# Edge stage of a graph kernel: zero columns widen the first layer's weights to 128, and one VectorE reduction over the three directions stands ahead of the flush

## The chip, the core and the metric

One NeuronCore of a Trainium2 chip runs the whole kernel as one program. Its engines run side by side, each with its own queue in program order, and wait for each other by semaphores: TensorE (PE, matmuls into PSUM), VectorE (DVE, elementwise and reductions), ScalarE (ACT), GpSimd (POOL, here mostly the issue of gathers and scatters) and SyncE (SP, which issues DMAs). The metric is the device time of one execution in microseconds (us), lower is better.

## What is computed

A layer over a graph of 6250 nodes with 256 features and 200000 edges sorted by their target: a layer norm, a graph convolution with a small network per edge, linear attention, and a mixture of eight experts. The part that matters here is the edge part of the convolution. Each edge has ten length features, from which two layers make 256 weights, and four attributes y. It fetches the row of its source node, 64 scalars g0 and 64 vectors g1 of three directions, and sends 512 values to its target node:

```python
h = jax.nn.silu(edge_length_embedded @ W_mlp1 / math.sqrt(N_BASIS))      # 10 -> 100
ew = h @ W_mlp2 / math.sqrt(N_HID)                                       # 100 -> 256
wa, wb, wc, wd = (ew[:, :MUL], ew[:, MUL:2 * MUL], ew[:, 2 * MUL:3 * MUL], ew[:, 3 * MUL:])
g0 = f0[edge_src]; g1 = f1[edge_src]
y0 = edge_attr[:, 0]; y1 = edge_attr[:, 1:4]
m0a = wa * g0 * y0[:, None]
m0b = wb * jnp.einsum('eum,em->eu', g1, y1) / math.sqrt(3.0)
m1a = wc[:, :, None] * g0[:, :, None] * y1[:, None, :]
m1b = wd[:, :, None] * g1 * y0[:, None, None]
s_mid = jax.ops.segment_sum(jnp.concatenate([m0a, m0b], axis=1), edge_dst, num_segments=N)
v_mid = jax.ops.segment_sum(jnp.concatenate([m1a, m1b], axis=1), edge_dst, num_segments=N)
```

The change touches `edge_length_embedded @ W_mlp1` and the `einsum` over the three directions m.

## The kernel before

The function `edges` works through 403 items. An item is 512 edges in four chunks of 128, one edge to a partition (GE = 512, GC = 4, MUL = 64, D = 256). Since edges are sorted, a chunk's targets lie in one block of 128 nodes, and the 49 blocks' sums stay in `acc` in SBUF. Items come in three phases, by how many blocks one spreads over: 355 items of one piece (the long phase), 35 of two pieces, 13 of four. In each phase a loop on the chip runs four items a turn, with buffers that rotate over two or four. The order on each engine is written out by hand, and the lead between engines is set by semaphore counts.

For item n the engines do this:

- SP loads the edges' records (`edge`) and the length features, transposed (`el`), which `prepare` and `nodes` have split in high and low parts, 30 rows of features in a tile of 128 partitions.
- POOL gathers the source nodes' rows, four indirect DMAs an item, into `rows[k]`.
- PE, `hidden` (L1005): the first layer, one matmul in rounded single precision. The stationary operand is `K.w_e1s`, 128 partitions by 100 columns, filled in its first 30 partitions by L335 and zero below; 512 edges stream past it into `ps_h`.
- ACT, `silu` (L876): reads 100 partitions of `ps_h` into `hT`.
- PE, `weights` (L1011): the second layer into `ps_e`, four full-precision matmuls, which the trace shows as two passes each.
- DVE, `one_hot` (L933): for each edge, where its target lies in its block. `by_attributes` (L942): g1 times y1, 768 products, into `dot3`, laid out as chunk, direction, channel. Channels lie side by side, so that one channel's three directions are 64 words apart. `second` (L948) adds directions 0 and 1 into `dot2`, and `third` (L952) adds direction 2 into `dot`. `products` (L958, L961, L965), called one item later, multiplies by the second layer's weights into `msg`. `flush` (L924) adds a finished block sum from PSUM (`ps_s`) to `acc`.
- ACT, `scalings` (L884) and `weighted` (L894): the parts that are scaled by one attribute per edge.
- PE, `sums` (L1024): the one-hot rows times the messages, into `ps_s`, for item n - 1.

In one turn, DVE runs: products of n - 1, one_hot of n, by_attributes of n, then the flushes. An item of the long phase has one flush, of n - 2, which waits for PE's sums of n - 2 (`summed`). The variable `at_end` says how many flushes stand ahead of the additions: at least one before. PE runs: weights of n, hidden of n + 1, sums of n - 1.

Some lines elsewhere are named by rows below. Two of them read SBUF with a step between elements. `place` (L1443, in `update`) is reduced over its eight experts with 11 words (44 bytes) from one to the next. The statistics that L381 subtracts are read with 6 words (24 bytes) between elements; L388 reads and writes the same number side by side. L1407 and L1472 reduce eight elements that lie side by side. L1700 is the experts' first layer, whose operands are rounded single precision, with 128 columns.

Of the kernel before, what the change touches and what calls it, by code (L numbers as in the profile page):

```python
# [19 lines left out]
P = 128  # L20
N_NODES, D, MUL = 6250, 256, 64
# [3 lines left out]
GE, GC = 512, 4  # L25
# [22 lines left out]
HID, BAS = 100, 10  # L48
# [14 lines left out]
f32, f32r, bf16, i32 = mybir.dt.float32, mybir.dt.float32r, mybir.dt.bfloat16, mybir.dt.int32  # L63
ALU, ACT, AX = mybir.AluOpType, mybir.ActivationFunctionType, mybir.AxisListType
# [49 lines left out]
class Mem:  # L114
# [5 lines left out]
    def sb(self, name, shape, dt=f32):  # L120
        return self.ctx.enter_context(self.nc.sbuf_tensor(f"{self.prefix}_{name}", shape, dt))
# [8 lines left out]
def prepare(nc, A, K):  # L130

    with ExitStack() as ctx:
        m = Mem(nc, ctx, "prepare")
        w_hi, low_row, w_part = m.sb("w_hi", [3 * BAS, HID], f32r), m.sb("low_row", [3 * BAS, 1]), m.sb("w_part", [3 * BAS, HID])
# [16 lines left out]
        made, scaled, d, summed, numbered, balanced = (m.sem(x) for x in (  # L151
            "made", "scaled", "vector_steps", "summed", "numbered", "balanced"))
# [84 lines left out]
        def _(dve):  # L237
            v, n = nc.vector, [0]
# [70 lines left out]
            spare = slice(2 * (QUADS + TWOS), NPAIR)  # L309
# [22 lines left out]
            nc.vector.scalar_tensor_tensor(w_part[:, :], w_hi[:, :].bitcast(f32), low_row[:, :], K.w_e1[:, :], ALU.mult,  # L332
                                           ALU.add).then_inc(scaled, 1)
            dve.wait_ge(scaled, 3)
            nc.vector.tensor_copy(K.w_e1s[0:3 * BAS, :], w_part[:, :]).then_inc(scaled, 1)  # L335
            nc.vector.tensor_scalar(K.sc_m[:, :], K.attr[:, :], C_S / 8.0, None, ALU.mult)
            dve.wait_ge(centred, 1)
            nc.vector.tensor_copy(K.w_kvT[:, :, 2 * D + E:], K.w_rc[:, :, :])
# [465 lines left out]
def edges(nc, A, K, acc):  # L804
# [3 lines left out]
    with ExitStack() as ctx:  # L808
# [3 lines left out]
        el, edge = four("el", [P, GE], f32r), four("edge", [P, GC, REC], i32)  # L812
        y = [e[:, :, 2:REC].bitcast(f32) for e in edge]
        hT = two("hT", [HID, GE])
        hot_y = two("hot_y", [P, GC, P])
        warm = m.sb("warm", [P, 1])
        spare = K.w_kvT[:, :, :].rearrange("p c n -> p (c n)")[:, 0:4 * D]
        dot3 = spare[:, 0:3 * GC * MUL].rearrange("p (c i u) -> p c i u", c=GC, i=3)
        dot2 = spare[:, 3 * GC * MUL:].rearrange("p (c u) -> p c u", c=GC)
        room = K.x2[:, :, :].rearrange("p t d -> p (t d)")  # L820
        rows = [room[:, k * GC * D:(k + 1) * GC * D].rearrange("p (c n) -> p c n", c=GC) for k in range(4)]
        left = room[:, 4 * GC * D:]
# [2 lines left out]
        dot = [left[:, k * GC * MUL:(k + 1) * GC * MUL].rearrange("p (c n) -> p c n", c=GC) for k in range(2)]  # L825
# [4 lines left out]
        loaded = [[m.sem(f"loaded_{ph.pieces}_{k}") for k in range(4)] for ph in PHASES]  # L830
        gathered = [m.sem(f"gathered{k}") for k in range(4)]
        c = {x: m.sem(x) for x in ("padded", "cleared", "messages", "flushed", "hidden", "act", "weights", "outer", "scaled",
                                   "hot_y", "dot3", "dot2", "dot", "hot", "summed", "passed")}
        block = ctx.enter_context(nc.Block())
        records = lambda ph: 16 * 3 * ph.pieces
        arrived = lambda ph, n, k: (loaded[PHASES.index(ph)][k], ph.loads(n, k, records(ph)))
# [73 lines left out]
        @block.vector  # L910
        def _(dve):
            v = nc.vector
            dve.sem_inc(c["messages"], FREE)
            dve.sem_inc(c["flushed"], FREE)
            for k in range(4):
                v.memset(el[k][:, :].bitcast(f32), 0.0).then_inc(c["padded"], 1)
            v.memset(acc[:, 0:(NB + 1) // 2, :], 0.0).then_inc(c["cleared"], 1)
            dve.wait_ge(c["cleared"], 2)

            def flush(n, k, ph, j, b):  # L920
                dve.wait_ge(c["flushed"], ph.seq(n) + (j + FREE))
                dve.wait_ge(c["summed"], ph.seq(n) + (j + 1 + AHEAD))
                a = acc[:, bass.ds(b, 1), :].rearrange("p a n -> p (a n)")
                v.tensor_tensor(a, a, ps_s[ph.bank(k, j)][:, :], ALU.add).then_inc(c["flushed"], 1)  # L924

            def homes(n, ph, pieces):
                return load_values(nc, mybir.EngineType.DVE, K.item_block, ph.seq(n) + pieces[0], len(pieces), NB)

            def one_hot(n, k, ph, j):
                at = slice(j * ph.len, (j + 1) * ph.len)  # L930
                if j == 0:
                    dve.wait_ge(*arrived(ph, n, k))
                v.scalar_tensor_tensor(hot[k][:, at, :], K.iota_f[:, :].unsqueeze(1).to_broadcast([P, ph.len, P]),  # L933
                                       K.item_base[:, bass.ds(ph.seq(n) + j, 1)],
                                       edge[k][:, at, 1:2].to_broadcast([P, ph.len, P]),
                                       ALU.add, ALU.is_equal).then_inc(c["hot"], 1)

            def by_attributes(n, k):
                dve.wait_ge(gathered[k], per(n, k, 64, 4))
                if not (isinstance(n, int) and n == 0):  # L940
                    dve.wait_ge(c["dot"], n)
                v.tensor_tensor(dot3[:, :, :, :], rows[k][:, :, MUL:D].rearrange("p c (i u) -> p c i u", i=3),  # L942
                                y[k][:, :, 1:4].unsqueeze(3).to_broadcast([P, GC, 3, MUL]),
                                ALU.mult).then_inc(c["dot3"], 1)

            def second(n):
                dve.wait_ge(c["dot3"], n + 1)
                v.tensor_tensor(dot2[:, :, :], dot3[:, :, 0, :], dot3[:, :, 1, :], ALU.add).then_inc(c["dot2"], 1)  # L948

            def third(n, k):  # L950
                dve.wait_ge(c["dot2"], n + 1)
                v.tensor_tensor(dot[k % 2][:, :, :], dot2[:, :, :], dot3[:, :, 2, :], ALU.add).then_inc(c["dot"], 1)  # L952

            def products(n, k):
                f, g = rows[k], msg[k % 2]
                w = ps_e[k % 2][:, :].rearrange("p (c b u) -> p c b u", c=GC, b=4)
                dve.wait_ge(c["weights"], n + 1)
                v.tensor_tensor(g.rearrange("p c (b u) -> p c b u", u=MUL)[:, :, 0:MSG // MUL:8, :],  # L958
                                f[:, :, 0:MUL].unsqueeze(2).to_broadcast([P, GC, 2, MUL]), w[:, :, 0:4:3, :],
                                ALU.mult).then_inc(c["outer"], 1)  # L960
                v.tensor_tensor(g[:, :, MUL:D].rearrange("p c (i u) -> p c i u", i=3),  # L961
                                f[:, :, MUL:D].rearrange("p c (i u) -> p c i u", i=3),
                                w[:, :, 1:2, :].to_broadcast([P, GC, 3, MUL]), ALU.mult)
                dve.wait_ge(c["dot"], n + 1)
                v.tensor_tensor(g[:, :, D:D + MUL], dot[k % 2][:, :, :], w[:, :, 2, :], ALU.mult).then_inc(c["messages"], 1)  # L965

            def body(n, k, of):
                if not (isinstance(n, int) and n < 1):
                    products(n - 1, (k - 1) % 4)
                for j in range(of(0).pieces):  # L970
                    one_hot(n, k, of(0), j)
                by_attributes(n, k)
                earlier, newer = [], []
                if not (isinstance(n, int) and n < 2):
                    earlier = [(n - 2, (k - 2) % 4, of(-2), j) for j in range(of(-2).early, of(-2).pieces)]
                if not (isinstance(n, int) and n < 1):
                    newer = [(n - 1, (k - 1) % 4, of(-1), j) for j in range(of(-1).early)]
                flushes = earlier + newer
                if flushes:
                    m, _, ph, j = flushes[0]  # L980
                    blocks = load_values(nc, mybir.EngineType.DVE, K.item_block, ph.seq(m) + j, len(flushes), NB)
                    flushes = [f + (b,) for f, b in zip(flushes, blocks)]
                at_end = max(len(earlier) if newer else len(earlier) - 1, 1)
                for f in flushes[:at_end]:
                    flush(*f)
                second(n)
                third(n, k)
                for f in flushes[at_end:]:
                    flush(*f)

            item_steps(dve, 0, NI, body, 2)
            products(NI - 1, (NI - 1) % 4)
            for n, first in ((NI - 2, ONE.early), (NI - 1, 0)):
                blocks = load_values(nc, mybir.EngineType.DVE, K.item_block, ONE.seq(n) + first, ONE.pieces - first, NB)
                for j, b in enumerate(blocks):
                    flush(n, n % 4, ONE, first + j, b)

        @block.tensor
        def _(pe):
            t = nc.tensor  # L1000

            def hidden(n, k, ph):

                pe.wait_ge(*arrived(ph, n, k))
                t.matmul(ps_h[k % 2][0:HID, :], K.w_e1s[:, :], el[k][:, :], start=True, stop=True).then_inc(c["hidden"], 1)  # L1005

            def weights(n, k):
                pe.wait_ge(c["messages"], n + 3)
# [853 lines left out]
def program(nc, A, out):  # L1862
    with ExitStack() as ctx:
# [16 lines left out]
        K.w_nodeA, K.w_nodeB = sb("w_nodeA", [P, 256]), sb("w_nodeB", [P, 256])  # L1880
        K.w_kvT, K.w_qT, K.w_projT = sb("w_kvT", [P, 2, 2 * D + 2 * E]), sb("w_qT", [P, 2, 256]), sb("w_projT", [P, 2, 256])
        K.w_e1, K.w_e2 = sb("w_e1", [3 * BAS, HID]), sb("w_e2", [HID, 256])
        K.w_e1s = sb("w_e1s", [P, HID], f32r)
        K.w_lo, K.w_rc, K.w_pr, K.b_pr = sb("w_lo", [P, 4, LO]), sb("w_rc", [P, 2, E]), sb("w_pr", [P, 2, E]), sb("b_pr", [P, E])
        K.z, K.std = sb("z", [P, NT, 2 * E]), sb("std", [P, NT])
        K.w_r, K.b_r, K.b_proj = sb("w_r", [P, 2, E]), sb("b_r", [P, E]), sb("b_proj", [P, D])
# [92 lines left out]
```

## Time and profile before

| | us |
|---|---|
| median of three runs | 3426.73 |
| lowest and highest | 3422.16, 3427.67 |
| the profiled execution | 3423.07 |
| its span, first to last instruction | 3421.3 |
| the long phase, from its first product to its last | 286.7 to 2207.9 |
| the phase of two pieces | 2213.3 to 2393.2 |
| the phase of four pieces | 2399.5 to 2492.1 |

A profile is one execution: 1.8 us of it lie around the span. A row names its line in the kernel before, the engine, the operation, the tiles written and read, and shapes as partitions by elements. PEld is PE's weight load, which overlaps its matmuls. The names in the trace are those of the memory that is used: `k_w_kvT` in the edge stage is the room of `dot3` and `dot2`, and `k_x` that of rows, messages, `dot` and one-hot rows. Matmul ends are modelled, and so is how early a matmul may seem to start; the starts of the weight loads are firmer. A DVE instruction that waits for nothing starts a little ahead of the recorded end of the one in front, so distances between starts add up, not durations. DVE's instructions without work in the tiles (register operations, loads of a table entry) run ahead beside the engine's work.

### The profile page before, as it was taken

The numbers are of one execution on the slowest core, as the hardware profiler recorded it, in microseconds if no ns is written. First come the engines' busy times: TensorE is split into PE (matmuls) and PEld (weight loads), VectorE is DVE, ScalarE is ACT, GpSimd is POOL, SyncE is SP. The second block draws the span as 40 slices with busy tenths as digits, with TensorE's granted clock in tenths as the row PEclk, the third lists the DMA queues.
The fourth block names the chain that finished last, engine by engine and source line by source line (L and its number), as shares of the span: only waits on it lengthen the run. The fifth ranks groups of instructions, "written<-read, shape, count | busy, mean of one in ns | idle before, by whom it ended". The sixth has DMA issues, their size and how long they took to land. (4 is left out here: it accounts for less than half of the span.)

```text
span 3421.3 us, 65304 instructions
## 1 busy us (share of the span) xinstructions
PE 3271.9 (96%) x15915; PEld 2833.8 (83%) x15915; DVE 2718.1 (79%) x5058; ACT 2630.4 (77%) x8258; POOL 2292.5 (67%) x2140
## 2 busy tenths in 40 slices
PE   5998999999999999999999999999789499999998
PEld 4886888888888888888888888888679388888887
DVE  7868889998889888898888988999967556656521
ACT  6667888888888888888888888888656367666742
POOL 5746777777777777777777777777527545445533
PEclk8998999999999999999999999999999799999999
DMA  6963333333333333333333333444348444545544
GB/s 221 308 228 98 111 110 111 110 110 110 110 111 111 111 110 110 111 111 111 110 110 111 111 111 110 110 109 108 84 118 160 140 119 139 144 117 143 141 109 132
DMA packets 322226, 431.91 MB, mean 126 GB/s; under 512 B 129227, under 2 KB 249751, under 8 KB 313943
## 3 DMA queue, kind: packets, MB, share of 16 engines
q0 software_dynamic: 105936, 253.72, 27.5%
q1 hardware_dynamic: 216199, 177.13, 17.6%
q8 instruction: 39, 0.64, 0.1%
q14 instruction: 52, 0.43, 0.0%
HBM read 366.03 MB, written 64.59 MB: 126 GB/s over the span
## 5 line engine op out<-in xcount | busy, mean ns | idle before, releaser
L864 POOL DMA_INDIRECT k_x<-gather_table,edges_edge x1612 | 1692.4, 1050 | 524.0 <-issue 493.8
L884 ACT ACTIVATE k_x<-k_x,edges_edge 128x64 f32<-128x64 f32 x4836 | 1196.8, 334 | 58.2 <-DVE k_x L958 54.8
L1024 PE MATMUL edges_ps_sum<-k_x,edges_hot_y 128*128 128x256 f32 x3224 | 961.9, 380 | 24.8 <-DVE accumulators L924 22.3
L1024 PE MATMUL edges_ps_sum<-k_x 128*128 128x256 f32 x3224 | 960.6, 380 | 0.0
L1011 PE MATMUL edges_ps_edge<-k_w_e,edges_hT 100*128 100x256 f32 x3224 | 765.4, 380 | 9.1 <-ACT edges_hT L876 9.1
L1024 PEld LDWEIGHTS edges_ps_sum<-k_x,edges_hot_y 128*128 128x128 f32 x3224 | 612.1, 190 | 131.3 <-DVE accumulators L924 19.3
L1011 PEld LDWEIGHTS edges_ps_edge<-k_w_e,edges_hT 100*128 100x128 f32 x3224 | 613.0, 190 | 96.2 <-issue 10.3
L1024 PEld LDWEIGHTS edges_ps_sum<-k_x 128*128 128x128 f32 x3224 | 613.2, 190 | 84.4
L894 ACT ACTIVATE edges_hot_y<-k_x,edges_edge 128x128 f32<-128x128 f32 x1612 | 514.2, 390 | 5.5 <-DVE k_x L933 5.3
L924 DVE TENSOR_TENSOR accumulators<-accumulators,edges_ps_sum 128x512 f32 x477 | 327.0, 686 | 162.4 <-PE edges_ps_sum L1024 158.1
L876 ACT ACTIVATE edges_hT<-edges_ps_hidden 100x512 f32<-100x512 f32 x403 | 240.0, 596 | 248.3 <-PE edges_ps_hidden L1005 247.9
L942 DVE TENSOR_TENSOR k_w_kvT<-k_x,edges_edge 128x768 f32<-128x768 f32 x403 | 386.5, 959 | 2.1 <-DMA k_x<-gather_table,edges_edge 2.1
L961 DVE TENSOR_TENSOR k_x<-k_x,edges_ps_edge 128x768 f32<-128x768 f32 x403 | 381.5, 947 | 0.0
L1778 ACT ACTIVATE experts_g<-experts_ps_h,weights_constants 128x512 f32<-128x512 f32 (+1 forms) x256 | 163.3, 638 | 255.1 <-PE experts_ps_h L1700 255.1
L1815 DVE TENSOR_TENSOR experts_g_lo<-experts_g,experts_g_hi 128x512 fp32r<-128x512 f32 x192 | 132.5, 690 | 226.9 <-ACT experts_g_hi L1778 226.9
L933 DVE SCALAR_TENSOR_TENSOR k_x<-k_iota_f,k_item_base,edges_edge 128x512 f32<-128x512 f32 (+2 forms) x477 | 309.7, 662 | 0.0
L1648 POOL DMA_INDIRECT out<-experts_y,weights_rows x112 | 198.8, 1775 | 157.1 <-DVE experts_y L1832 125.0
L958 DVE TENSOR_TENSOR k_x<-k_x,edges_ps_edge 128x512 f32<-128x512 f32 x403 | 276.6, 686 | 28.4 <-issue 0.2
L1638 POOL DMA_INDIRECT k_x<-tokens,weights_rows x112 | 129.4, 1155 | 233.6 <-DMA weights_rows<-slots 184.2
L1005 PE MATMUL edges_ps_hidden<-edges_el,k_w_e1s 128*100 128x512 f32 x403 | 236.6, 587 | 6.6 <-DMA edges_el<-el_parts 6.6
L952 DVE TENSOR_TENSOR k_x<-k_w_kvT 128x256 f32<-128x256 f32 x403 | 171.3, 425 | 13.7
L948 DVE TENSOR_TENSOR k_w_kvT<-k_w_kvT 128x256 f32<-128x256 f32 x403 | 168.6, 418 | 0.1
(329 smaller groups left out, 4362.5 us busy)
## 6 DMA issues: line engine op xcount, KB each, us to landing
k_x<-in_w SPq DMA_DIRECT2D x64, 1024.0 KB, 7.0
k_x<-gather_table,edges_edge POOLq DMA_INDIRECT x1612
el_parts<-nodes_el_parts SPq DMA_DIRECT2D x41, 384.0 KB, 3.5
edges_el<-el_parts SPq DMA_DIRECT2D x355, 40.0 KB
edges_el<-el_parts SPq DMA_DIRECT2D x425, 20.0 KB
nodes_el<-in_el SPq DMA_DIRECT2D x41, 192.0 KB, 3.9
k_x<-in_x SPq DMA_DIRECT2D x7, 896.0 KB, 11.1
residual<-nodes_res SPq DMA_DIRECT2D x49, 128.0 KB, 3.5
```

The lines of the kernel that those rows point to most:

```text
L864: nc.gpsimd.indirect_dma_start(out=rows[k][:, j, :], out_offset=None, in_=K.table_d.rearrange("t p d -> (t p) d"), in_offset=bass.Indirect ...
L876: nc.scalar.activation(hT[k % 2][:, :], ps_h[k % 2][0:HID, :], ACT.Silu, scale=1 / math.sqrt(BAS)).then_inc(c["act"], 1)
L884: x = nc.scalar.activation(g[:, j, D + MUL * (i + 1):D + MUL * (i + 2)], g[:, j, 2 * D:MSG], ACT.Identity, scale=y[k][:, j, 1 + i:2 + i])
L894: x = nc.scalar.activation(hot_y[k % 2][:, j, :], hot[k][:, j, :], ACT.Identity, scale=y[k][:, j, 0:1])
L924: v.tensor_tensor(a, a, ps_s[ph.bank(k, j)][:, :], ALU.add).then_inc(c["flushed"], 1)
L933: v.scalar_tensor_tensor(hot[k][:, at, :], K.iota_f[:, :].unsqueeze(1).to_broadcast([P, ph.len, P]), K.item_base[:, bass.ds(ph.seq(n) + j, ...
L942: v.tensor_tensor(dot3[:, :, :, :], rows[k][:, :, MUL:D].rearrange("p c (i u) -> p c i u", i=3), y[k][:, :, 1:4].unsqueeze(3).to_broadcast ...
L958: v.tensor_tensor(g.rearrange("p c (b u) -> p c b u", u=MUL)[:, :, 0:MSG // MUL:8, :], f[:, :, 0:MUL].unsqueeze(2).to_broadcast([P, GC, 2, ...
L961: v.tensor_tensor(g[:, :, MUL:D].rearrange("p c (i u) -> p c i u", i=3), f[:, :, MUL:D].rearrange("p c (i u) -> p c i u", i=3), w[:, :, 1: ...
L1005: t.matmul(ps_h[k % 2][0:HID, :], K.w_e1s[:, :], el[k][:, :], start=True, stop=True).then_inc(c["hidden"], 1)
L1011: x = t.matmul(ps_e[k % 2][:, j * 256:(j + 1) * 256], hT[k % 2][:, j * P:(j + 1) * P], K.w_e2[:, :], start=True, stop=True)
L1024: x = t.matmul(into[:, o * D:(o + 1) * D], rows_hot[:, j, :], msg[k % 2][:, j, o * D:(o + 1) * D], start=j % ph.len == 0 and o == 0, stop= ...
```

## The change

Three edits. The stationary operand of the first layer gets 28 more columns, all zero, and the matmul writes 128 partitions of `ps_h` rather than 100; ACT still reads 100. The additions `second` and `third` become one `tensor_reduce` over `dot3`, viewed with the direction innermost. And `at_end` may be zero, so that in the long phase the flush stands behind the reduction.

```diff
-            nc.vector.tensor_copy(K.w_e1s[0:3 * BAS, :], w_part[:, :]).then_inc(scaled, 1)
+            nc.vector.tensor_copy(K.w_e1s[0:3 * BAS, 0:HID], w_part[:, :]).then_inc(scaled, 1)
...
-        dot2 = spare[:, 3 * GC * MUL:].rearrange("p (c u) -> p c u", c=GC)
...
-            def second(n):
+            def over_directions(n, k):
                 dve.wait_ge(c["dot3"], n + 1)
-                v.tensor_tensor(dot2[:, :, :], dot3[:, :, 0, :], dot3[:, :, 1, :], ALU.add).then_inc(c["dot2"], 1)
-
-            def third(n, k):
-                dve.wait_ge(c["dot2"], n + 1)
-                v.tensor_tensor(dot[k % 2][:, :, :], dot2[:, :, :], dot3[:, :, 2, :], ALU.add).then_inc(c["dot"], 1)
+                v.tensor_reduce(dot[k % 2][:, :, :], dot3.rearrange("p c i u -> p c u i"), AX.X, ALU.add).then_inc(c["dot"], 1)
...
-                at_end = max(len(earlier) if newer else len(earlier) - 1, 1)
+                at_end = max(len(earlier) if newer else len(earlier) - 1, 0)
                 for f in flushes[:at_end]:
                     flush(*f)
-                second(n)
-                third(n, k)
+                over_directions(n, k)
                 for f in flushes[at_end:]:
                     flush(*f)
...
-                t.matmul(ps_h[k % 2][0:HID, :], K.w_e1s[:, :], el[k][:, :], start=True, stop=True).then_inc(c["hidden"], 1)
+                t.matmul(ps_h[k % 2][:, :], K.w_e1s[:, :], el[k][:, :], start=True, stop=True).then_inc(c["hidden"], 1)
...
-        K.w_e1s = sb("w_e1s", [P, HID], f32r)
+        K.w_e1s = sb("w_e1s", [P, P], f32r)
```

On DVE, in the loop of the long phase, from the products by attributes of one item to the first product with the weights. The rows are before's, then after's; L799 loads a table entry, and `accumulators` is `acc`:

```order
L942 TENSOR_TENSOR k_w_kvT<-k_x,edges_edge 128x768 [waits edges_dot,edges_gathered3]
L799 ISA
L799 TENSOR_LOAD k_item_block
L921 REGISTER_ALU
L924 ISA [waits edges_summed,edges_flushed]
L924 TENSOR_TENSOR accumulators<-accumulators,edges_ps_sum 128x512
L948 TENSOR_TENSOR k_w_kvT<-k_w_kvT 128x256 [waits edges_dot3]
L952 TENSOR_TENSOR k_x<-k_w_kvT 128x256 [waits edges_dot2]
L958 TENSOR_TENSOR k_x<-k_x,edges_ps_edge 128x4x2x64 [waits edges_weights]
```

```order
L941 TENSOR_TENSOR k_w_kvT<-k_x,edges_edge 128x768 [waits edges_dot,edges_gathered3]
L799 ISA
L799 TENSOR_LOAD k_item_block
L947 TENSOR_REDUCE k_x<-k_w_kvT 128x256 [waits edges_dot3]
L920 REGISTER_ALU
L923 ISA [waits edges_summed,edges_flushed]
L923 TENSOR_TENSOR accumulators<-accumulators,edges_ps_sum 128x512
L953 TENSOR_TENSOR k_x<-k_x,edges_ps_edge 128x4x2x64 [waits edges_weights]
```

The wait for `summed` and the flush behind it have moved past the addition over directions, which waits only for `dot3`, DVE's own product just in front.

On DVE, in the loop of the two-piece phase, from the first flush of an item to the next item's first product, before and after:

```order
L924 TENSOR_TENSOR accumulators<-accumulators,edges_ps_sum 128x512
L947 REGISTER_ALU
L948 TENSOR_TENSOR k_w_kvT<-k_w_kvT 128x256 [waits edges_dot3]
L952 TENSOR_TENSOR k_x<-k_w_kvT 128x256 [waits edges_dot2]
L921 REGISTER_ALU
L924 ISA [waits edges_summed,edges_flushed]
L924 TENSOR_TENSOR accumulators<-accumulators,edges_ps_sum 128x512
```

```order
L923 TENSOR_TENSOR accumulators<-accumulators,edges_ps_sum 128x512
L946 REGISTER_ALU
L947 TENSOR_REDUCE k_x<-k_w_kvT 128x256 [waits edges_dot3]
L920 REGISTER_ALU
L923 ISA [waits edges_summed,edges_flushed]
L923 TENSOR_TENSOR accumulators<-accumulators,edges_ps_sum 128x512
```

Here nothing has changed its place: one flush ahead of the addition, one behind it. PE's order is the same in both kernels.

## Rows read from the trace of the kernel before

**Rows 1.** Page, part 1: busy us, share of the span, instructions.

```profile
PE 3271.9 (96%) x15915; PEld 2833.8 (83%) x15915; DVE 2718.1 (79%) x5058; ACT 2630.4 (77%) x8258; POOL 2292.5 (67%) x2140
```

**Rows 2.** By window: length, busy of PE, PEld, DVE, ACT, POOL (count), PEclk, DMA.

```profile
1000.00:1500.00 500.00, 500.00 (x2310) 436.02 (x2309) 449.95 (x740) 436.63 (x1569) 387.54 (x370) 1.00 0.40 111
...
2208.00:2397.00 189.00, 189.00 (x874) 164.77 (x873) 186.77 (x347) 163.88 (x592) 143.34 (x137) 1.00 0.41 109
2397.00:2500.00 103.00, 78.25 (x329) 62.69 (x329) 91.55 (x180) 59.43 (x220) 50.02 (x48) 0.97 0.27 70
```

**Rows 3.** Waits from 300 to 2200 us: us in total, times, longest.

```profile
ACT edges_hT L876 <- PE edges_ps_hidden L1005: 240.0, 351, 0.7
DVE accumulators L924 <- PE edges_ps_sum L1024: 150.9, 351, 0.5
```

**Rows 4.** DVE's timeline, one long-phase item: start us, us, what, [idle before].

```profile
1503.87 0.69 DVE L958 TENSOR_TENSOR k_x<-k_x,edges_ps_edge 128x512 f32<-128x512 f32 x1
...
1506.33 0.97 DVE L942 TENSOR_TENSOR k_w_kvT<-k_x,edges_edge 128x768 f32<-128x768 f32 x1
1507.67 0.69 DVE L924 TENSOR_TENSOR accumulators<-accumulators,edges_ps_sum 128x512 f32 x1 [0.37 <-PE edges_ps_sum L1024]
1508.28 0.42 DVE L948 TENSOR_TENSOR k_w_kvT<-k_w_kvT 128x256 f32<-128x256 f32 x1
1508.73 0.42 DVE L952 TENSOR_TENSOR k_x<-k_w_kvT 128x256 f32<-128x256 f32 x1
1509.29 0.69 DVE L958 TENSOR_TENSOR k_x<-k_x,edges_ps_edge 128x512 f32<-128x512 f32 x1
```

**Rows 5.** L958 in the long and the two-piece phase: durations, first and last start.

```profile
L958 DVE TENSOR_TENSOR k_x<-k_x,edges_ps_edge x356: 680/687/689, 286.7 to 2207.9; 128x512 f32<-128x512 f32 x178
...
L958 DVE TENSOR_TENSOR k_x<-k_x,edges_ps_edge x34: 677/679/689, 2213.3 to 2393.2; 128x512 f32<-128x512 f32 x34
```

**Rows 6.** Timeline of DVE, one item of the two-piece phase.

```profile
2348.22 0.41 DVE L948 TENSOR_TENSOR k_w_kvT<-k_w_kvT 128x256 f32<-128x256 f32 x1
...
2349.02 0.68 DVE L924 TENSOR_TENSOR accumulators<-accumulators,edges_ps_sum 128x512 f32 x1
2349.61 0.68 DVE L958 TENSOR_TENSOR k_x<-k_x,edges_ps_edge 128x512 f32<-128x512 f32 x1
```

**Rows 7.** Reductions by shape: busy us, mean ns of one, idle time before.

```profile
L1443 DVE TENSOR_REDUCE update_where<-k_w_qT 128x10 f32<-128x80 f32 x7 | 2.1, 295 | 0.2
...
L1407 DVE TENSOR_REDUCE update_best<-k_iota_f 128x5 f32<-128x40 f32 x7 | 1.4, 197 | 0.2
...
L1472 DVE TENSOR_REDUCE k_w_e<-k_item_start 1x40 f32<-1x320 f32 x1 | 0.5, 474 | 0.0
L1443 DVE TENSOR_REDUCE update_where<-k_w_qT 128x6 f32<-128x48 f32 x2 | 0.5, 232 | 0.1
...
L1407 DVE TENSOR_REDUCE update_best<-k_iota_f 128x3 f32<-128x24 f32 x2 | 0.4, 177 | 0.1
```

**Rows 8.** The same view: reads with a step (L381) and side by side (L388).

```profile
L381 DVE TENSOR_TENSOR first_diff<-first_stats 128x49 f32<-128x49 f32 x1 | 0.2, 245 | 0.0
...
L388 DVE SCALAR_TENSOR_TENSOR first_var<-first_var,first_diff 128x49 f32<-128x49 f32 x1 | 0.2, 211 | 0.0
```

**Rows 9.** Timeline around the hidden layer; the experts' first layer, its weight load.

```profile
1508.87 0.17 PEld L1005 LDWEIGHTS edges_ps_hidden<-edges_el,k_w_e1s 128*100 128x100 f32 x1
...
1509.09 0.42 PEld L1024 LDWEIGHTS edges_ps_sum<-k_x,edges_hot_y 128*128 128x128 f32 x2
...
1509.32 0.59 PE L1024 MATMUL edges_ps_sum<-k_x,edges_hot_y 128*128 128x256 f32 x2
...
3000.14 0.39 PE L1700 MATMUL experts_ps_h<-experts_x_lo,experts_w_hi 128*128 128x512 f32 x1
3000.37 0.39 PE L1700 MATMUL experts_ps_h<-experts_x_hi,experts_w_lo 128*128 128x512 f32 x1
...
L1700 PEld LDWEIGHTS experts_ps_h<-experts_x_hi,experts_w_hi 128*128 128x128 f32 x384 | 72.7, 189 | 18.9 <-DVE experts_x_lo L1808 4.5
```

More of the change, by code:

```diff
@@ L832, in edges @@
         c = {x: m.sem(x) for x in ("padded", "cleared", "messages", "flushed", "hidden", "act", "weights", "outer", "scaled",
-                                   "hot_y", "dot3", "dot2", "dot", "hot", "summed", "passed")}
+                                   "hot_y", "dot3", "dot", "hot", "summed", "passed")}
         block = ctx.enter_context(nc.Block())
```

## The prediction

> **What bounds the kernel now.** The page's totals come first: TensorE (PE) is busy 96% of the span, VectorE (DVE) 79% [rows 1]. The share is an average over stages, so the table by windows comes next. From 1000 to 1500 us, in the middle of the edge stage, PE is busy all 500 us at granted clock 1.00 (the 2.4 GHz level), and DVE 449.95 us. In the two short phases behind it DVE is busy 186.77 of 189 and 91.55 of 103 us [rows 2]. So the edge stage has two limits: PE in its long phase of whole items, and DVE, all but full, in the phases of two and four pieces.
>
> The waits say how much room DVE has in the long phase. Between 300 and 2200 us PE stands in none of the waits. DVE waits 150.9 us for the sums that `flush` adds, 351 times, and ACT 240.0 us for the hidden layer [rows 3]. The timeline of one item shows where: the product L942 starts at 1506.33 and ends at 1507.30, then DVE is idle for 0.37 until the sums of item n-2 are done, flushes at 1507.67, adds at 1508.28 (L948) and 1508.73 (L952), and starts the next item's products (L958) at 1509.29, 5.42 us after the last start at 1503.87 [rows 4]. Over the long phase 356 starts of L958 lie between 286.7 and 2207.9 us, 5.41 us apart. In the two-piece phase 34 starts are 5.45 us apart [rows 5].
>
> **The two additions become one reduction.** L948 (0.42) and L952 (0.42) go, with the `dot2` hand-over between them. What comes is one `tensor_reduce` over 768 elements in, 256 out. Its input is `dot3` read with the direction innermost, and two directions of one channel lie 64 words, 256 bytes, apart. Its time D is the question of this change, and no row has this form. Both ends come from the nearest rows.
> - If the step costs nothing: reductions whose input lies side by side, L1407, take 177 ns for 24 elements and 197 for 40, and L1472 474 for 320, so 277/280 = 0.99 ns for each further element [rows 7]. That gives 197 + 728 x 0.99 = 0.92 us. The three-direction products, 768 elements, take 0.95 to 0.97 [rows 4]. I take 0.95 as this end.
> - If every step to another place costs: L1443 reduces with elements 44 bytes apart, and takes 232 ns for 48 and 295 for 80, so 63/32 = 1.97 ns an element, twice the other rate [rows 7]. That gives 295 + 688 x 1.97 = 1.65 us. With exactly twice the 1.04 ns by which the first additions (0.42 for 256) and the products (0.95 for 768) differ, (0.95 - 0.42)/512, it is 295 + 688 x 2.07 = 1.72.
>
> A second family of rows speaks for the step as the cause, not the reduction: L381 subtracts two columns of a table that has 24 bytes from element to element, 245 ns for 49 elements, while L388 with its elements side by side takes 211 [rows 8]. That is 34 ns more for 49 elements, near one more DVE step each less a smaller fixed part. The steps seen are 24 and 44 bytes and both cost; 256 bytes is farther, not nearer, so I take D = 1.70 us, between 1.60 and 1.80.
>
> Two pages of the Trainium skill pull apart here. "Advanced Engine Details and Errata", section "SBUF Cachelines", says that an access pattern needs at least two hits on a 16-byte line to run at full rate, which 24, 44 and 256 bytes all miss; by that rule the sum would be the forecast below, and the rows of L1443 agree. "VectorE: DVE Perf Modes", section "The perf-mode tier table", puts `tensor_reduce` at one element a cycle like an fp32 `tensor_tensor`, with no word on the step; by that rule it would be the first rival, and only the rows with side-by-side input agree.
>
> **The sum for DVE in the long phase.** The order shows that the reduction now stands straight behind L942, and the flush behind it, so that the 0.37 of waiting is filled by work. One item of DVE without any wait is then:
> - L958 to the start of L942: 1506.33 - 1503.87 = 2.46 [rows 4];
> - L942 with the hand-over of `dot3`: 0.97 + 0.03, the 0.03 being the gap between the end of L948 at 1508.70 and L952, which has the same kind of wait [rows 4]: 1.00;
> - the reduction until the flush starts: D less the 0.08 by which a follower that waits for nothing starts ahead of the recorded end (the flush of 0.69 is followed after 0.61) [rows 4]: 1.62;
> - the flush until the next L958: 0.60, from 2349.02 to 2349.61 [rows 6].
> Together 5.68 us, against the 5.41 that PE needs. DVE becomes the bound, by 0.27 us an item. 355 items: **+96 us**. The point from which DVE decides is D = 1.43. Had the additions stayed two, this order would give 2.46 + 1.00 + 0.80 + 0.60 = 4.86 and nothing on the path.
>
> Does a ring through the other engines need more than 5.68? ACT is held by its own work for 5.42 less the 0.68 that it waits per item (240.0/351) [rows 3], 4.74 us. The flush of item n-2 waits for sums that PE starts a whole item earlier, and PE's sums wait for a flush one item older still. Neither closes before DVE.
>
> **The two short phases.** There DVE is the bound already, and the order around the additions is as before: one or two flushes ahead, the others behind. From L948 to the next flush is 2349.02 - 2348.22 = 0.80 [rows 6]. It becomes D - 0.08 = 1.62, so +0.82 on each of 35 + 13 = 48 items: **+39 us**. PE's own waits there are for DVE, and grow with it.
>
> **The first layer with 128 columns.** PE's array takes 512 moving columns as before; only the weight load grows, from 0.17 us for 100 columns [rows 9] to the 0.19 of the other loads of 128 columns, rounded single-precision ones too (L1700, 189 ns) [rows 9]. It lies beside a matmul: one PE slot is 500/2310 = 0.216 us [rows 2]. The hidden layer's slot is 0.23, from 1509.09, where the next weights start, to 1509.32, and the experts' matmuls of the same type with full 128 columns are also 0.23 apart, 3000.14 to 3000.37 [rows 9]. So I take nothing; the bounds are 403 x 0.015 = 6 us gained, if the slot fell to 0.216, and 403 x 0.02 = 8 us lost, if the longer load showed. Both count only while PE is the bound, which it then is not. The zero columns' outputs land in rows of PSUM that no one reads. The Trainium skill ("TensorE: Matmul & The Clock Gate", "Weight-path perf modes") loads full 128-column weights faster when they aren't FP32; L1700's 189 ns shows no such thing for this type, and by that rule the sum would be no other, as the load is hidden.
>
> The order on the other queues is untouched. SP and POOL wait for `messages` and `scaled`, which follow DVE's pace: POOL's four gathers an item are not the bound: among the waits of the long phase none is for them [rows 3]. The wider weights are cleared once, ahead of everything.
>
> **Sum.** 96 + 39 = +135 us on the profiled 3423.07: 3558. The median of the runs is 3.7 above that execution, so I forecast **3562 us**. With D = 1.60 it is 0.17 x 355 + 0.72 x 48 = +95, with D = 1.80 0.37 x 355 + 0.92 x 48 = +175: 3522 to 3602 for this case.
>
> **Rivals.**
> 1. The step costs nothing (D = 0.95). DVE's item is 4.93, PE stays the bound, the long phase doesn't move. The short phases pay (0.95 - 0.08 - 0.80) x 48 = +3 us, and the wider weights give back up to 6: 3424 to 3430, no difference that can be told. For it: the L1407 and L1472 rows. Against it: L1443, which is the only reduction here with a step in SBUF, and L381. 0.14.
> 2. Part of the step is hidden, because three addresses return to neighbouring words for the next channel (D from 1.1 to 1.5). The long phase pays nothing up to D = 1.43. At 1.3: 0.42 x 48 = +20, so 3447; at 1.5: 0.07 x 355 + 0.62 x 48 = +55, so 3481. 0.06.
> 3. A step of 256 bytes is dearer than one of 44, by a third DVE step an element: D = 295 ns + 688 x 3.1 = 2.43 us, item 6.41, +1.00 x 355 + 1.55 x 48 = +429, 3856. Nothing in the rows shows that the price grows with the step. 0.04.
> 4. Rival 1 with more than 6.9 us saved on PE: the slot would have to fall by more than 0.015. 0.02.
>
> **How the numbers follow.** My forecast has 0.74. The range has to reach down through rival 2 to leave out 0.20: 3450 to 3610. 0.2% of this kernel, 7 us, is about what a measurement can tell from no change. Slower by more: 0.74 + 0.06 + 0.04 = 0.84; within it 0.14; faster 0.02.
>
> **What would show it.** Right: the reduction's row has 1.6 to 1.8 us; the flush has no idle time ahead of it; starts of the first product are 5.6 to 5.8 apart in the long phase, and DVE has next to no idle time there, while PE's busy share falls below 100%. Wrong at its root: the reduction takes under 1.43 us. Wrong in the sum: D as said, but DVE still waits, or its other operations change their times. For the weights: the load's row reads 0.19 and the slot around the hidden layer stays 0.23.

## The result and the profile after

| | before | after |
|---|---|---|
| median of 20 runs each, us | 3426.22 | 3430.09 |
| ratio, 95% interval | | 1.0017 (1.001 to 1.0023) |
| profiled execution, its span | 3423.07, 3421.3 | 3427.01, 3425.3 |

The kernel is 0.17% slower: less than the 0.2% that the forecast called no change, though twenty runs of each put it clear of zero. The forecast was 3562 us, 4% slower, within 3450 to 3610. The change that it forecast is 35 times the one measured, and the measured time lies below its range. One of the eleven executions of the kernel below that has the additions back in its short phases took 9232 us; its ratio is worked out without that one (median 3424.65).

The difference lies in the duration of the reduction, which takes 1.03 us and not 1.70. First the page's part 5 after, and the waits from 300 to 2200 us, which answer [rows 3]:

```profile
L947 DVE TENSOR_REDUCE k_x<-k_w_kvT 128x256 f32<-128x768 f32 x403 | 416.0, 1032 | 12.3
...
ACT edges_hT L875 <- PE edges_ps_hidden L999: 239.9, 351, 0.7
DVE k_x L953 <- PE edges_ps_edge L1005: 119.2, 351, 0.3
```

DVE no longer waits for the sums ahead of the flush. It waits for PE's second layer instead, ahead of the item's first product, 351 times as before, for 119 us rather than 151. DVE's timeline after, one item, answers [rows 4]; the last two rows are of the two-piece phase:

```profile
1504.50 0.69 DVE L953 TENSOR_TENSOR k_x<-k_x,edges_ps_edge 128x512 f32<-128x512 f32 x1 [0.34 <-PE edges_ps_edge L1005]
...
1506.96 0.95 DVE L941 TENSOR_TENSOR k_w_kvT<-k_x,edges_edge 128x768 f32<-128x768 f32 x1
1507.95 1.03 DVE L947 TENSOR_REDUCE k_x<-k_w_kvT 128x256 f32<-128x768 f32 x1
1508.90 0.68 DVE L923 TENSOR_TENSOR accumulators<-accumulators,edges_ps_sum 128x512 f32 x1
...
2347.55 0.68 DVE L923 TENSOR_TENSOR accumulators<-accumulators,edges_ps_sum 128x512 f32 x1
2348.15 0.68 DVE L953 TENSOR_TENSOR k_x<-k_x,edges_ps_edge 128x512 f32<-128x512 f32 x1
```

Read by starts: 2.46 from the first product to the products by attributes, 0.99 to the reduction, 0.95 to the flush. From a flush to the next item's first product it is 0.60 where DVE waits for nothing, as in the two-piece phase. That makes 5.00 in all. PE needs 5.42. Starts of the first product in the long phase (without its last one), in the two-piece and in the four-piece phase; the first two answer [rows 5]:

```profile
L953 DVE TENSOR_TENSOR k_x<-k_x,edges_ps_edge x355: 675/687/689, 286.9 to 2203.1; 128x512 f32<-128x512 f32 x178
...
L953 DVE TENSOR_TENSOR k_x<-k_x,edges_ps_edge x34: 667/669/686, 2213.9 to 2398.5; 128x512 f32<-128x512 f32 x34
...
L953 DVE TENSOR_TENSOR k_x<-k_x,edges_ps_edge x13: 678/680/681, 2404.8 to 2498.4; 128x512 f32<-128x512 f32 x13
```

The long phase runs at 5.41 us an item, as before. In the two-piece phase 33 steps take 184.6 us, against 179.9: 5.59 an item rather than 5.45. The last item's first product starts at 2498.4 rather than 2492.1, 6.3 us later, which is within the interval of the ratio (3.4 to 7.9 us). The span is only 4.0 longer. The missing 2.3 lie behind the edge stage, in code that didn't change: from that start to the span's end it is 926.9 us here and 929.2 before, and between 925.8 and 933.2 in the nine kernels, with and without the change, that run the same code there. DVE's busy time by windows answers [rows 2]: 465.29 of 500 us in the long phase, up from 449.95, and 188.59 of 189 in the two-piece one, up from 186.77.

```profile
1000.00:1500.00 500.00, 500.00 (x2310) 438.15 (x2309) 465.29 (x647) 436.46 (x1568) 387.25 (x370) 1.00 0.40 111
2208.00:2397.00 189.00, 189.00 (x854) 159.59 (x852) 188.59 (x305) 157.39 (x577) 145.80 (x134) 1.00 0.40 106
```

### The profile page after: what moved, and what is told of

The parts are those of the page before. It is cut to its first block and busy times, and to the rows that moved or that the text cites. A ratio compares the mean times of both kernels' runs of the same rounds, so it can differ in the third digit from the quotient of the medians.

```text
span 3425.3 us, 64989 instructions
## 1 busy us (share of the span) xinstructions
PE 3275.3 (96%) x15915; PEld 2841.0 (83%) x15915; DVE 2786.1 (81%) x4655; ACT 2628.4 (77%) x8258; POOL 2298.4 (67%) x2140
## 5 line engine op out<-in xcount | busy, mean ns | idle before, releaser
L947 DVE TENSOR_REDUCE k_x<-k_w_kvT 128x256 f32<-128x768 f32 x403 | 416.0, 1032 | 12.3
L999 PE MATMUL edges_ps_hidden<-edges_el,k_w_e1s 128*128 128x512 f32 x403 | 236.5, 587 | 6.4 <-DMA edges_el<-el_parts 6.4
L960 DVE TENSOR_TENSOR k_x<-k_x,edges_ps_edge 128x256 f32<-128x256 f32 x403 | 166.5, 413 | 0.0
```

The lines of the kernel that those rows point to most:

```text
L947: v.tensor_reduce(dot[k % 2][:, :, :], dot3.rearrange("p c i u -> p c u i"), AX.X, ALU.add).then_inc(c["dot"], 1)
```

## The experiments

**Was the sum right and only the duration wrong?** One addition of 576 elements on DVE ahead of each reduction, whose result nothing reads, makes up what the reduction lacked of 1.70.

```diff
                 dve.wait_ge(c["dot3"], n + 1)
+                v.tensor_tensor(filler[:, :], spare[:, 0:576], spare[:, 0:576], ALU.add)
                 v.tensor_reduce(dot[k % 2][:, :, :], dot3.rearrange("p c i u -> p c u i"), AX.X, ALU.add)...
```

> The changed kernel with one addition over 576 elements on DVE ahead of each reduction, its result read by no one. It stands for a reduction that takes 0.67 us more, that is 1.70 us, the duration the prediction had assumed. In the changed kernel DVE's item without waits is 2.46 + 0.99 + 0.95 + 0.60 = 5.00 us against PE's 5.42. If the sum of the prediction was right and only the duration was wrong: 5.00 + 0.67 = 5.67, +0.25 x 355 + 0.67 x 48 = +121 us over the changed kernel, so 3551 us, ratio to before 1.036. If DVE has more room than the sum says (its gaps hide part of it): under 1.02. If a ring through other engines closes: over 1.045.

Measured: 3545.45 us, ratio 1.0358 (1.0342 to 1.0374). The starts in the long phase:

```profile
L955 DVE TENSOR_TENSOR k_x<-k_x,edges_ps_edge x356: 672/680/692, 288.6 to 2296.2; 128x512 f32<-128x512 f32 x178
...
1000.00:1500.00 500.00, 494.40 (x2213) 412.72 (x2212) 496.97 (x708) 408.16 (x1501) 392.35 (x354) 1.00 0.38 106
```

355 steps in 2007.6 us are 5.655 us an item, against the 5.67 of the sum. The second row is the window from 1000 to 1500 us: DVE is busy 496.97 of 500, and PE falls to 494.40. The sum and its bound held, and no longer chain of waits through other engines showed.

**Where is the point from which DVE decides?** The same with 264 elements.

> As the filler run, with an addition over 264 elements, whose result no one reads, ahead of each reduction. It lasts 0.35 us from start to start. The sum of the prediction puts the point from which DVE decides in the long phase at 5.42 - 5.00 = 0.42 us more than the changed kernel has. So the long phase stays at 5.42 us an item and only the 48 items of the short phases pay: 0.35 x 48 = +17 us over the changed kernel, about 3443, ratio 1.0065. If the point lies lower (DVE needs some slack to keep PE fed), the long phase rises too: at half the slack 355 x 0.14 = 50 us more, ratio 1.02.

Measured: 3449.23 us, ratio 1.0071 (1.0057 to 1.0086). The starts in the long and in the two-piece phase, and the window from 1000 to 1500 us:

```profile
L955 DVE TENSOR_TENSOR k_x<-k_x,edges_ps_edge x356: 675/687/689, 288.1 to 2210.7; 128x512 f32<-128x512 f32 x178
...
L955 DVE TENSOR_TENSOR k_x<-k_x,edges_ps_edge x34: 675/682/683, 2216.1 to 2411.9; 128x512 f32<-128x512 f32 x34
...
1000.00:1500.00 500.00, 500.00 (x2310) 438.21 (x2309) 496.81 (x740) 437.08 (x1572) 387.54 (x370) 1.00 0.40 110
```

1922.6/355 = 5.416 in the long phase: 0.35 us of work more an item cost nothing there, with 0.07 left. In the two-piece phase 195.8/33 = 5.93, 0.34 up on the changed kernel. DVE is busy 496.81 of 500 us in the long phase and PE still all 500, so 0.07 us of slack an item is enough.

**Where does the small loss come from?** The additions are put back in the two short phases alone.

```diff
-            def over_directions(n, k):
+            def over_directions(n, k, ph):
                 dve.wait_ge(c["dot3"], n + 1)
+                if ph.pieces > 1:
+                    v.tensor_tensor(dot2[:, :, :], dot3[:, :, 0, :], dot3[:, :, 1, :], ALU.add).then_inc(c["dot2"], 1)
+                    dve.wait_ge(c["dot2"], n + 1 - QUADS)
+                    v.tensor_tensor(dot[k % 2][:, :, :], dot2[:, :, :], dot3[:, :, 2, :], ALU.add).then_inc(c["dot"], 1)
+                    return
...
```

> The changed kernel, but in the two short phases (35 + 13 items) the two additions are back, so that the reduction stands in the long phase alone. Theory 1, the loss of the changed kernel is the 0.15 us by which the reduction is longer (0.95 from start to start, against 0.80 for the two additions) on the 48 items where DVE is the bound: these items fall back to 5.45 us in the two-piece phase, and the ratio to before is 1.000 (within 0.0007), 6 us under the changed kernel. Theory 2, the loss comes from the long phase (the later flush, or the wider weights): the ratio stays at 1.0017.

Measured: 3425.82 us, ratio 1.0001 (0.9992 to 1.0011). In the two-piece phase:

```profile
L959 DVE TENSOR_TENSOR k_x<-k_x,edges_ps_edge x34: 678/680/686, 2213.8 to 2393.5; 128x512 f32<-128x512 f32 x34
```

179.7/33 = 5.45, as before. Reduction, later flush and wider weights all stay in for 355 items and cost nothing that can be told; the loss was the reduction in the 48 items of the short phases.

**The parts alone.** First the 128 columns.

> The kernel before with the first layer's weights widened to 128 columns and nothing else. Theory 1: the hidden layer's slot on PE doesn't change (0.23 us from the next weight load to the next matmul), the load takes 0.19 rather than 0.17 beside another matmul, ratio 1.000. Theory 2, the slot shrinks to the 0.216 of the other matmuls: 5.40 us an item in the long phase, 6 us gained, ratio 0.998. Theory 3, the longer load shows: 8 us lost, 1.002.

Measured: 3424.97 us, ratio 1.0006 (0.9996 to 1.0017). The interval leaves out the 0.998 of theory 2, and the 1.002 of theory 3 only narrowly. The trace says more: the long phase keeps 5.41 us an item, and the load takes 190 ns in the window from 1000 to 1500 us, where it took 167 before:

```profile
L1005 PEld LDWEIGHTS edges_ps_hidden<-edges_el,k_w_e1s 128*128 128x128 f32 x93 | 17.7, 190 | 2.4
...
1509.96 0.19 PEld L1005 LDWEIGHTS edges_ps_hidden<-edges_el,k_w_e1s 128*128 128x128 f32 x1
1510.18 0.43 PEld L1024 LDWEIGHTS edges_ps_sum<-k_x,edges_hot_y 128*128 128x128 f32 x2
```

The next weight load starts 0.22 us later, as before (1508.87 and 1509.09), so the longer load lies beside a matmul, and the slot didn't shrink either. Theories 2 and 3 are out.

Then the later flush, in the kernel before:

```diff
-                at_end = max(len(earlier) if newer else len(earlier) - 1, 1)
+                at_end = max(len(earlier) if newer else len(earlier) - 1, 0)
```

> The kernel before, with its two additions and 100 columns, in which only the flush of the long phase goes behind the additions. DVE's item without waits is 2.46 + 1.00 + 0.80 + 0.60 = 4.86 us against PE's 5.42. The wait of 0.37 us ahead of the flush disappears, and one of some 0.5 us comes ahead of the next first product, for PE's second layer. Theory 1: nothing moves, 5.416 us an item, ratio 1.000 (within 0.001). Theory 2, the later flush costs something at the phase borders or frees PE somewhere: a difference of over 0.1%.

Measured: 3425.15 us, ratio 1.0005 (0.9996 to 1.0014), and 5.41 us an item in the long phase. The wait moved as expected (waits from 300 to 2100 us):

```profile
DVE k_x L958 <- PE edges_ps_edge L1011: 160.9, 332, 0.5
```

**Why is the reduction cheap?** A block in which DVE alone reduces data in SBUF, in many shapes, stands between the edge stage and the next. `side` takes groups of r elements side by side. `apart` takes g groups of r elements that lie s words apart, while the groups are neighbours.

```diff
+            def side(g, r, op=ALU.add):
+                done(v.tensor_reduce(to[:, 0:g], flat[:, 0:g * r].rearrange("p (g r) -> p g r", r=r), AX.X, op))
+
+            def apart(g, r, s, op=ALU.add, src=flat, at=0):
+                done(v.tensor_reduce(to[:, 0:g], src[:, at:at + r * s].rearrange("p (r s) -> p s r", r=r)[:, 0:g, :], AX.X, op))
...
```

> The changed kernel with one more block between the edge stage and the next, in which DVE alone runs some 50 small reductions and additions on SBUF data, twice over, each waiting for the one before; the other engines stand still. Only their durations count, not the time of the run (some 25 us longer). The changed kernel's reduction took 1.03 us, 1.04 ns an element, though its three directions are 256 bytes apart, while L1443 of the kernel before took 1.97 ns for each further element at 44 bytes. Theory A, the step itself costs but only some steps: groups of 8 with 44 bytes rise by 2 ns an element here too, and groups with 256 bytes by 1 ns, so a step that keeps to whole 64 bytes is free. Theory B, the step never costs and L1443 is slowed by what the other engines do at its time: all forms rise by 1.0 ns an element, and 10 groups of 8 at 44 bytes take 0.20 us, like 10 groups side by side (0.24 at most). Theory C, the number of steps in a group counts, since three addresses come back to the neighbouring word soon: 8 at 256 bytes rise by 2 ns an element, 3 at 256 bytes by 1 ns, and between 3 and 16 it turns. In all of them the copy of the edge stage's form (4 x 64 groups of 3) takes 1.03.

Measured, groups by shape with mean ns. L1061 is `side`, L1064 `apart`, and L1088 a copy of the edge stage's form. The L1064 rows shown have a step of 256 bytes:

```profile
L1064 DVE TENSOR_REDUCE probe_to<-k_x 128x64 f32<-128x768 f32 x2 | 2.9, 1452 | 0.1
...
L1088 DVE TENSOR_REDUCE probe_to<-k_w_kvT 128x256 f32<-128x768 f32 x2 | 2.1, 1032 | 0.1
L1064 DVE TENSOR_REDUCE probe_to<-k_x 128x64 f32<-128x512 f32 x2 | 2.1, 1027 | 0.1
L1061 DVE TENSOR_REDUCE probe_to<-k_x 128x256 f32<-128x768 f32 x2 | 1.9, 954 | 0.1
L1064 DVE TENSOR_REDUCE probe_to<-k_x 128x40 f32<-128x320 f32 x2 | 1.4, 697 | 0.1
L1061 DVE TENSOR_REDUCE probe_to<-k_x 128x64 f32<-128x512 f32 x2 | 1.4, 686 | 0.1
...
L1061 DVE TENSOR_REDUCE probe_to<-k_x 128x40 f32<-128x320 f32 x2 | 1.0, 487 | 0.1
```

Groups of 8 with a step take 1027 ns for 64 groups where 686 are needed side by side: 5.3 ns more a group. 256 groups of 3 take 1032 against 954: 0.3 ns a group. Ten groups of 8 take 285 to 291 ns at 44, 48, 64, 128 and 256 bytes alike. So theory A, by which some steps are free for their size, is out. Theory B is out too: from 2511 to 2544 us, the time of this block, no other engine is busy, and L1443's form still costs more than side by side. It costs 1.6 ns an element for its sizes, and 1.72 for larger ones, (1027 - 697)/192, rather than 1.97. What is left is the number of steps in a group.

The second block asks what about that number counts. `lines` is `apart` with the groups q words from each other.

```diff
+            def lines(g, r, s, q):
+                a = flat[:, 0:r * s].rearrange("p (r g q) -> p g r q", r=r, q=q)[:, 0:g, :, 0]
+                done(v.tensor_reduce(to[:, 0:g], a, AX.X, ALU.add))
...
```

> The changed kernel with the same kind of block of DVE reductions as before, again read by their durations alone (the run is longer by the block). The first table showed, beyond the 1.04 ns an element of side-by-side input: groups of 8 at any step from 44 to 256 bytes cost 5.2 ns more a group, groups of 12 7.8, groups of 16 10.2, but groups of 3 only 0.3. Theory R (revisits): what costs is to go to another 16 bytes than those read just before; a few such lines stay at hand, so with 3 steps each line serves four groups, with 8 it is lost before the next group comes. Then groups of 3 whose neighbours are 16 bytes apart (each access a new line) cost some 0.65 ns an element more, 64 groups about 125 ns, and groups of 8 cost the same with neighbours 4, 8, 16 or 32 bytes apart. Between 3 and 8 steps there is a turn within one or two sizes. Theory G (group): every element of a group past the third or so costs 0.65 ns more, whatever was read before: groups of 3 cost nothing with neighbours 16 or 32 bytes apart either, and the extra of groups of 2 to 8 rises in a straight line from 3 on.

Measured, 64 groups each, side by side (L1061) and with a step of 256 bytes (L1064) in turn, from the timeline, for groups of 3, 4 and 8:

```profile
2510.62 0.35 DVE L1061 TENSOR_REDUCE probe_to<-k_x 128x64 f32<-128x192 f32 x1
2511.01 0.37 DVE L1064 TENSOR_REDUCE probe_to<-k_x 128x64 f32<-128x192 f32 x1
2511.41 0.42 DVE L1061 TENSOR_REDUCE probe_to<-k_x 128x64 f32<-128x256 f32 x1
2511.87 0.59 DVE L1064 TENSOR_REDUCE probe_to<-k_x 128x64 f32<-128x256 f32 x1
...
2516.76 0.69 DVE L1061 TENSOR_REDUCE probe_to<-k_x 128x64 f32<-128x512 f32 x1
2517.48 1.03 DVE L1064 TENSOR_REDUCE probe_to<-k_x 128x64 f32<-128x512 f32 x1
```

Groups of 3 pay 0.02 us for 192 elements, groups of 4 pay 0.17 for 256, 0.65 ns an element, and all larger ones pay about that rate too (8: 0.34/512). That is a jump between 3 and 4, not a line that rises from 3. And groups of 3 whose neighbours are 8, 16 and 32 bytes apart, rather than 4; the last row has neighbours at 4 bytes again:

```profile
2519.73 0.43 DVE L1068 TENSOR_REDUCE probe_to<-k_x 128x64 f32<-128x192 f32 x1
2520.20 0.50 DVE L1068 TENSOR_REDUCE probe_to<-k_x 128x64 f32<-128x192 f32 x1
2520.73 0.49 DVE L1068 TENSOR_REDUCE probe_to<-k_x 128x64 f32<-128x192 f32 x1
...
2530.16 0.37 DVE L1064 TENSOR_REDUCE probe_to<-k_x 128x64 f32<-128x192 f32 x1
```

At 16 bytes every access goes to 16 bytes not read before, and the groups of 3 pay as well: 0.15 us, 0.76 ns an element, near the 125 ns that theory R gave. Theory G is out. In `lines` the step inside a group grows with the distance of the neighbours, to 1024 bytes at 16, but the step isn't the reason: the last row has that step too, and takes 0.37 us. The cost rises from neighbours at 4 bytes over 8 to 16 and no further at 32, which is why the unit is taken to be 16 bytes. The reading that fits all these rows is theory R: what costs is a read from 16 bytes that aren't among the three read last. `dot3` with its three directions reads each of its three places four times in turn. That the engine keeps such places is inferred from the durations alone.

**Can both reads and writes be had side by side?** `dot3` as chunk, channel, direction: the product writes with a step of 12 bytes, and the reduction reads without.

> The changed kernel with the three products of a channel side by side in dot3, so that the reduction reads without a step and the product L941 writes with a step of 12 bytes. By the first table the reduction falls from 1.03 to 0.95 us, and the product rises by 75 ns for every 256 elements, 0.22 us, to 1.17 (seen for one addition over 256 elements written at 12 bytes: 499 ns against 424). So DVE's item is 0.14 us longer: nothing in the long phase (5.14 against 5.42), +7 us in the short phases, ratio to before 1.0037. If writing with a step is free where three passes fill the same places, the product stays at 0.95, 0.08 x 48 = 4 us come back and the ratio is 1.0006.

Measured: 3437.82 us, ratio 1.0039 (1.0027 to 1.0051). In the long phase, 1000 to 1500 us, and DVE's waits for gathered rows in the two-piece phase, 2215 to 2408 us:

```profile
L941 DVE TENSOR_TENSOR k_w_kvT<-k_x,edges_edge 128x768 f32<-128x768 f32 x93 | 112.4, 1209 | 0.0
L947 DVE TENSOR_REDUCE k_x<-k_w_kvT 128x256 f32<-128x768 f32 x93 | 88.6, 953 | 3.2
...
DVE k_w_kvT L941 <- DMA k_x<-gather_table,edges_edge: 3.9, 6, 0.7
```

The reduction fell by 0.08, and the product rose from 0.95 to 1.21, a little more than expected. The item of the two-piece phase rose by 0.26 us in the mean. Of this, 0.13 is the two operations by their starts: 27 of the 33 steps are 5.70 to 5.75 us long, against 5.59. The other six are 6.40 to 6.53 long, because DVE waits there for gathered rows, 3.9 us in all, 0.12 an item. In the changed kernel such a wait came once in this phase, for 0.4 us. Whether the new layout brings these waits about or this one execution is not shown.

**An attempt at a better kernel.** On top of the later flush, the four-piece phase runs flush, addition, flush, addition, flush, flush.

> The same, and in the four-piece phase the four flushes of an item are spread: flush, addition, flush, addition, flush, flush. Two flushes in a row are 0.82 us apart there, since the second waits for the first, but 0.60 when another operation follows. Theory 1, DVE's own chain is the bound of this phase as of the two-piece one: an item falls by 0.22 us or a little more, from 7.63 to 7.4, 13 items, 3 us less, ratio 0.999. Theory 2, the phase hangs on a ring between PE and DVE (PE waits for a flush to free a bank, DVE for the sums): bringing the second flush behind an addition delays PE and nothing is gained or 0.1 us an item is lost, ratio 1.000.

Measured: 3425.22 us, ratio 1.0004 (0.9994 to 1.0014). The first items of the phase wait for other engines and take up to 10.8 us here and 10.4 before, so the last nine are compared. Here are their first products, before and in this kernel, and this kernel's waits for the sums from 2431 to 2496 us:

```profile
L958 DVE TENSOR_TENSOR k_x<-k_x,edges_ps_edge x9: 678/680/680, 2433.2 to 2492.1; 128x512 f32<-128x512 f32 x9
...
L958 DVE TENSOR_TENSOR k_x<-k_x,edges_ps_edge x9: 679/681/682, 2435.7 to 2494.3; 128x512 f32<-128x512 f32 x9
...
DVE accumulators L924 <- PE edges_ps_sum L1032: 1.9, 8, 0.3
```

An item takes 58.6/8 = 7.33 us rather than 58.9/8 = 7.36: 0.03 of the 0.22 came. The rest is waiting. Ahead of an item's third and fourth flush together DVE is now idle for 0.38 us, where it was 0.14 before, and the row shows part of it as waits for PE's sums, eight times; the kernel before waits for them once in its last nine items. That fits theory 2, the ring between PE and DVE, though no run tests it by itself. No version here is faster than the kernel before.

## Why the prediction was wrong, point by point

- **The bound of each phase:** right. PE bounds the long phase and DVE the short ones; the filler runs moved each as the sum said.
- **The reduction's duration D:** the step that failed. The sum took 1.70 us and it is 1.03. The prediction had both ends of the bound, 0.95 and 1.65 to 1.72, and chose by "both cost; 256 bytes is farther, not nearer". That compared the size of the step, which turned out not to matter, and passed over that L1443 comes back to its first place after eight steps and `dot3` after three. L381, the second family, read each place once. Neither row was near in what counts.
- **The upper end itself:** too high as well. 64 groups of 12 at 256 bytes, 768 elements that all pay, took 1.45 us. With that D the prediction's own formula gives 0.02 x 355 + 0.57 x 48 = 34 us, a time of 3461 and not 3562. The 1.97 ns an element came from two sizes of L1443; the same forms alone gave 1.6, and larger ones 1.72.
- **The range:** the interval of D, 1.60 to 1.80, was drawn around one end. Rival 2 named the mechanism that the runs bear out, three addresses that return to neighbouring words, but with a D of 1.1 to 1.5, and got 0.06. Rival 1, 3424 to 3430, met the time within 0.1 us and got 0.14. Its D of 0.95 was near, but its reason, that a step costs nothing, holds only nearly, and only for groups of three. The Trainium skill ("Advanced Engine Details and Errata", "SBUF Cachelines") asks for two hits on a line of 16 bytes; with three lines in turn, `dot3` has four hits on each, so the rule did not say what the prediction read out of it.
- **The rest of DVE's item:** 2.46 + 1.00 + 0.60 forecast, 2.46 + 0.99 + 0.60 found. With D = 1.03 the same formula gives nothing in the long phase and (1.03 - 0.08 - 0.80) x 48 = +7 us; the edge stage ended 6.3 us later.
- **The later flush and the 128 columns:** nothing each, as forecast. The 6 us that the columns might have gained were never there: the prediction's slot of 0.23 runs from a load's start to a matmul's, and from load to load the hidden layer's slot was 0.22 already before.

## What to carry to other kernels

When the one new duration of a change decides between two bounds, and its nearest rows disagree by a factor of 1.8, the forecast has two cases, and the likelier one should not get three quarters unless the rows share what makes the cost. Ask of a strided read how many places it visits before it comes back, not how long its step is. And an engine with 0.4 us of slack an item takes 0.35 us more without a trace of it in the time of that phase, while the same work costs in full in a short phase where that engine is already the bound.

## What the runs showed of the hardware

- DVE reads fp32 from SBUF nearly at its side-by-side rate of 1.04 ns an element also with a step, as long as a group has up to three elements and the groups are neighbours: 256 groups of 3 took 1032 ns with a step, side by side 954. With four or more every element costs about 0.65 ns more (64 groups of 4: 585 to 420 ns, of 8: 1027 to 686). For groups of 8 this is the same at steps from 44 to 256 bytes.
- Groups of 3 pay too, 0.76 ns an element, when neighbouring groups lie 16 bytes apart (64 groups: 0.50 us to 0.35).
- Writing with a step costs too: the product of 768 elements took 1.21 us at 12 bytes, 0.95 side by side.
- A weight load of 128 columns in rounded single precision took 190 ns, like the full-precision ones; 100 columns took 167 ns.
